# A table of positions in a fused attention and mixture-of-experts kernel: tile 3's columns are turned at position 16, the q/k product of tile 1 moves to 18

## The reference, cut to what matters

```python
# attention, per sequence
q, k, v = split(x @ w_qkv.T)            # 16 heads x 16
q, k = rms_norm(q), rms_norm(k)         # over the 16 of a head
q, k = rope(q), rope(k)
attn = softmax(mask(q @ k.T * scale))   # causal, 512 x 512
x = layernorm(x + (attn @ v) @ w_proj.T)
# feed-forward
normed = x * rsqrt(mean(x * x) + 1e-8) * norm_weight
shared = relu(normed @ sw1 + sb1) @ sw2 + sb2
probs = sigmoid(normed @ router_w.T)
scores, idx = top_k(probs, 2); w = scores / (sum(scores) + 1e-6)
routed = sum over the two experts e of  w_e * (relu(normed @ ew1[e] + eb1[e]) @ ew2[e] + eb2[e])
x = layernorm(x + shared + routed)
```

## Time and profile before

| | us |
|---|---|
| median of 3 runs | 946.98 (946.95 to 947.47) |
| the profiled execution | 943.19 |
| its span, first to last instruction | 941.4 |
| mean granted TensorE clock | 0.986 |
| TensorE busy | 880.8 (94%) |
| VectorE busy | 581.1 (62%) |
| ScalarE busy | 613.8 (65%) |
| GpSimd busy | 433.2 (46%) |

### The profile page before, as it was taken

The page is one execution under the profiler, slowest core; times in us unless marked ns, Lnnn a source line. Parts: engine busy times, 40 slices in busy tenths (PEclk is TensorE's granted clock), DMA queues, the critical chain, the costliest instruction groups (busy, mean ns, idle before and its releaser), DMA issues.

```text
span 941.4 us, 26114 instructions
## 1 busy us (share of the span) xinstructions
PE 880.8 (94%) x9049; PEld 698.1 (74%) x9050; DVE 581.1 (62%) x1206; ACT 613.8 (65%) x1061; POOL 433.2 (46%) x602
## 2 busy tenths in 40 slices
PE   4678999999999979999999999999999999999997
PEld 1444556565555647888888989989899889898886
DVE  8664878989988737784444544444444432437976
ACT  4678988888888767343565655556655454666764
POOL 5342454777868636572234434354434344512311
PEclk8799999999999999999999999999999999999999
DMA  5122142425212256567882122121212111239751
GB/s 178 68 68 68 68 147 91 155 84 198 97 70 75 81 185 226 199 211 264 254 293 73 56 68 67 46 70 54 68 48 76 46 58 48 77 118 291 221 168 56
DMA packets 68705, 112.76 MB, mean 120 GB/s; under 512 B 7728, under 2 KB 46000, under 8 KB 68496
## 3 DMA queue, kind: packets, MB, share of 16 engines
q1 hardware_dynamic: 51248, 77.32, 25.0%
q10 hardware_dynamic: 10896, 16.40, 5.9%
q0 software_dynamic: 6480, 17.97, 5.3%
HBM read 66.58 MB, written 45.08 MB: 119 GB/s over the span
## 4 chain that ended last, share of the span: by engine, by line
PE 68%; POOL 9%; issue 7%; DVE 7%; ACT 7%; DMA 1%; another core or an unknown queue 0%; ACTq 0%; DVEq 0%; POOLq 0%; SPq 0%
PE hb L1884 25%; PE yb L1903 24%; ACT prob L871 3%; PE pv_bank L1668 3%; PE hb L1734 3%; PE yb L1771 3%; PE tr L1754 2%; PE slot L1642 2%; POOL rsum L699 1%; PE ma L1681 1%; POOL rsum L696 1%; POOL xg_rows L740 1%; PE slot L1655 1%; POOL nat L714 1%; PE mb L1818 1%
## 5 line engine op out<-in xcount | busy, mean ns | idle before, releaser
L1043 ACT ACTIVATE hf<-hb,b 128x256 f32<-128x256 f32 (+1 forms) x392 | 154.8, 453 | 205.1 <-PE hb L1884 184.8
L1884 PE MATMUL hb<-xgT,wts 128*128 128x256 f16 (+1 forms) x1872 | 213.3, 263 | 1.7 <-ACT hf L1043 1.4
L1903 PE MATMUL yb<-wts,hh 128*128 x1704 | 210.5, 273 | 0.6 <-DVE hh L1472 0.6
L1472 DVE TENSOR_TENSOR hh<-hf,hh 128x1024 f16<-128x1024 f32 (+1 forms) x98 | 118.8, 1215 | 133.8 <-ACT hh L1048 117.6
L1884 PEld LDWEIGHTS hb<-xgT,wts 128*128 x1872 | 181.3, 98 | 20.8 <-issue 1.2
L806 POOL DMA_INDIRECT y_tok<-yb,dest x71 | 77.7, 1095 | 224.1 <-DVE yb L1484 207.3
L1903 PEld LDWEIGHTS yb<-wts,hh 128*128 128x128 f16 x1704 | 166.4, 98 | 19.3 <-DVE hh L1472 1.0
L871 ACT ACTIVATE prob<-slot 128x1024 f32<-128x1024 f32 x160 | 156.4, 1041 | 34.7 <-PE slot L1655 32.1
L1048 ACT ACTIVATE hh<-hf 128x1024 f16<-128x1024 f32 (+1 forms) x98 | 97.6, 996 | 3.1
L740 POOL DMA_INDIRECT xg_rows<-xnh,sl_i x64 | 74.8, 1168 | 15.5 <-issue 13.1
L1484 DVE SCALAR_TENSOR_TENSOR yb<-yb,b2bc 128x512 f32<-128x512 f32 (+1 forms) x39 | 25.1, 643 | 86.4 <-PE yb L1903 52.0
(11 more groups left out here) (250 smaller groups left out, 1437.6 us busy)
## 6 DMA issues: line engine op xcount, KB each, us to landing
wts<-in_w_all SPq DMA_DIRECT2D x23, 512.0 KB
wts<-y_tok SPq DMA_DIRECT2D x32, 256.0 KB, 4.5
xg<-xg_rows ACTq DMA_DIRECT2D x30, 264.0 KB
stage<-in_w_all SPq DMA_DIRECT2D x12, 512.0 KB
w_split<-chunk_hl SPq DMA_DIRECT2D x12, 512.0 KB
xTf<-in_xT SPq DMA_DIRECT2D x8, 512.0 KB
xin<-in_x SPq DMA_DIRECT2D x8, 512.0 KB
resid<-y SPq DMA_DIRECT2D x16, 256.0 KB
```

What stands on the lines that cost most here:

```text
L1043: act.activation(hf[:, c, 0:size], hb[c // 2][:, (c % 2) * TT:(c % 2) * TT + size], ACT.Relu, bias=bias, scale=1.0 / WS).then_inc(S("relu_ ...
L1472: dve.tensor_tensor(hh[:, par, 1, cs, 0:size], hf[:, cs, 0:size], hh[:, par, 0, cs, 0:size], ALU.subtract).then_inc(S("h_lo"), 1)
L1884: ins = pe.matmul(hb[hc // 2][:, (hc % 2) * TT:(hc % 2) * TT + size], weights(e, c, w, hc * P, P), xgT[:, par, x * DC + c, 0:size], start= ...
L1903: ins = pe.matmul(bank, hh[:, par, x, hc, P * j:P * j + P], weights(e, DC + hc * D // CH, w, hc * D % CH, D), start=(n == 0), stop=(n == H ...
```

## The change

Only numbers in the tables of positions change. For batches 2 to 7, modulo 20: the q/k product of tile 1 goes from 16 to 18 and its rotation from 17 to 19; the roots of tiles 0 and 1 and what follows them (`REFINE`, `QN`) go one position later; the turning of tile 3 goes from 18 to 16, in batch 1 as well; the turning of tile 0 goes from 6 to 7; the rank from 16 to 17 (offset 56 to 57), because the turned k columns of tile 3 now use `mc` at 16; the first scatters and the tables follow by one position.

```diff
-QK = (-28, -24, -20, -16)
-ROPE = (-27, -23, -19, -15)
-ROOT = (-21, -12)
-REFINE = (-20, -11)
+QK = (-28, -22, -20, -16)
+ROPE = (-27, -21, -19, -15)
+ROOT = (-20, -12)
+REFINE = (-19, -11)
 MORE_WEIGHTS = -24
-QN = (-20, -18, -11, -10)
-TR = (-14, -10, -6, -2)
+QN = (-19, -17, -11, -10)
+TR = (-13, -10, -6, -4)
...
-RANK = (56,)
-SCATTER = (58, 59, 61, 63)
+RANK = (57,)
+SCATTER = (59, 60, 61, 63)
...
-SPACED = (58, 60, 64, 66)
+SPACED = (59, 60, 64, 66)
...
-TABLE = NPOS * (NB - 1) + 57
+TABLE = NPOS * (NB - 1) + 58
...
 OPENING = {
...
-    TR: ((-33, -28, -27, -26), (7, 10, 14, 18)),
+    TR: ((-33, -28, -27, -26), (7, 10, 14, 16)),
```

## The result

The changed kernel takes 968.75 us (median of four runs, 967.51 to 974.34) against 946.97 us. The ratio is 1.0243, 95% interval 1.0215 to 1.0271. The prediction named 949.4 us, range 943.0 to 953.4: the sign was right, the size was not, and the time lies outside the range.

What follows compares the result with a forecast made beforehand. Attention windows were taken as set by handovers, VectorE's list closing four of five; the routed experts are TensorE's own. Opening −3.0, windows +4.4, end +1.0 make +2.4 us: 949.4 us median, range 943.0 to 953.4.

Steps and rivals of the forecast that it cites:

- The opening: Second batch's first scores: TensorE's 1.94 us wait for the k copies goes; −3.0 us, bounds −1.2 to −3.6.
- The clock's share of this term: Opening, 82 to 84 us: if the half clock follows from the pause, it goes too; 1.63 us on two products.
- The windows, rotation: Third to seventh batch: tile 1's rotation moves behind the projection on VectorE; +1.20 in four windows, −0.4 in the fifth, sum +4.4.
- the square's wait of 2.5 us: Windows, ScalarE: `sq` (L888) waits for tile 1's `ssq`, one buffer, about 2.5 us, five times.
- the wait for the roots: Windows, VectorE: `nt` (L1176) newly waits for ScalarE's `ry`; 0.75 us taken, 0 to 1.4.
- my loop: Four windows of five: projection, VectorE's list, last attended tile, TensorE, projection; work added on VectorE there costs its full length.
- The windows, GpSimd: Windows, GpSimd: `norms` and two scatters now come ahead of tile 2's swap; left to the first rival.
- POOL becomes the bound: Slower rival, windows: VectorE waits 1.1 to 2.0 us for tile 2's swap; +3.2 us, 952.6; chance 0.26 with the lost opening.
- The end of the stage: End of attention: token count moves behind both early hidden pieces, tables begin 2.45 us later; +1.0 us, between +0.3 and +2.1.
- the operation that I guessed would lose its 1.8 us: L1340 in VectorE's tables, 1.95 us where some 0.15 is due; whatever holds it may be over: −1.8 us.
- VectorE absorbs the move: Faster rival, windows: `nat` regains 0.51 us beside the swap, windows −0.4; total −3.1, 943.9 us; chance 0.32.
- putting rope behind a piece of `shifted`: Windows: by the shared-port rule rope waits about half of `shifted`'s 2.48 us; four windows 5 us dearer, 954.4; counted with slower rival.

Runs made afterwards that it cites:

- rank late with the scatters kept: Kernel before with rank and tables one position later and the scatters at their old positions, first at 58: 1.0049, 947.7 us.
- the scatters of batch 4 apart: Changed kernel with each of batch 4's 8 scatters waiting for the exponentials of batch 7 to reach its place: 1.0192, 963.1 us.
- The change with the scatters kept: Changed kernel with the scatters back at their old positions, from 58, rank and all else staying changed: 1.0169, 959.1 us.

## Why the prediction was wrong, point by point

**The opening** (−3.0 us) was right in place and nearly in size: −2.4 us (0.13 to 0.37%) alone. The pause of the earlier trace rows is gone in the changed kernel; TensorE there:

```profile
82.87 1.46 PE L1681 MATMUL ma<-wqkv,xTh 128*128 128x512 f16 x6 [0.24 <-ACT sq L888]
84.25 2.36 PE L1668 MATMUL pv_bank<-prob,vst 128*32 128x512 f32 x32
```

Both products, 2.69 and 2.76 us in the earlier trace rows, are back at the full clock's lengths. The clock's share of this term (1.63 us) isn't there in every execution: of six profiles with the old opening, all with the pause of 1.94 us, three (rotation late, scatters late, rank late with the scatters kept) have the full clock behind it.

**The windows, rotation** (+4.4 us) had the right mechanism and half the size: +9 us alone. With the changed order around it, and the scatters kept, it is more: 16 us above the kernel before, although that has the opening's gain in it. The order of VectorE, the square's wait of 2.5 us and the wait for the roots came as written. Two pieces were missing. I counted ScalarE's late square as covered by its idle time and overlooked that it holds bank `ma`: TensorE's v product waits for it (1.05 us in the window shown, 5.1 us in five windows; none in these windows before, and 1.8 us in the run with the late rotation alone). And the pause at the attended tile falls on an earlier tile than the one of the earlier trace rows, so my loop, which carried only the last tile's wait, was not the one that closed. That loop also left out TensorE's wait for tile 0's high half, which was as large before (2.8 us in five waits) as the one for `an` (2.8 in four).

**The windows, GpSimd.** Beside the size of the rotation's term, this is the step that failed: the sum gave the scatter's move nothing. "POOL becomes the bound" was a rival with 0.26, priced at +3.2 us by the wait for tile 2's swap alone. That wait came in the changed kernel (1.78 us). The scatter's move costs 19 us by itself, half of it through tile 0's high half, which I had not followed, and 7 us in the changed kernel, of which the run without the stall (the scatters of batch 4 apart) already gives 5 back. The earlier trace rows showed the swap ending at 215.29 and a full queue; what I did not ask is where on GpSimd the scatter had stood before: in idle time, where it was free.

**The price of a pause** was taken as its length. In the changed kernel pauses of 1.6 to 2.5 us at `an` had the lower clock behind them in four windows, and the attended product lost 1.2 to 1.7 us in each (4.05 for 2.36 in the one shown). I had used this at the opening, as a gain, and not in the windows, as a cost.

**The stall at the seventh end** (6 us) was in the profile before, as 3.46 us on ScalarE, and I had no term for it.

**The end of the stage** (+1.0 us) agrees with +1.0 us alone, whose interval (−0.3 to +2.5) can't tell that size from nothing or from twice as much. The count and the tables of the changed kernel, and the operation that I guessed would lose its 1.8 us:

```profile
442.19 0.15 DVE L1330 COPY cum<-mc 1x8 f32<-1x8 f32 x1 [2.50 <-PE mc L1715]
...
443.85 0.15 DVE L1340 SCALAR_TENSOR_TENSOR cum<-seg,iota_e 1x8 f32<-1x8 f32 x1
```

VectorE waits 2.50 us for the count, and L1340 takes 0.15 us, so the 1.8 us did come back: `hh` begins 9.2 us behind the first of these operations where it was 11.3. That the whole change loses 6 us behind the last projection is more than this term; the scatters alone have 3.5 us there (962.1 − 406.5 against 552.1), the late rank with the scatters kept 2.7. What makes these is not shown.

**The rivals.** "VectorE absorbs the move" was wrong. The Trainium skill's rule on the shared port ("SBUF — State Buffer", section "Who interferes with whom") was read in the prediction as putting rope behind a piece of `shifted`; the trace doesn't show that: `rot` at 214.35 takes 0.69 us and `ssq` follows at once, beside `shifted` from 214.54. If one of them was held, it was `shifted`: 2.51 us for two, where two take 1.11 us at 206.46 in the same kernel.

The pieces measured alone are +1.98% (scatters), +0.97% (rotation), +0.49% (rank and tables, scatters kept) and −0.25% (opening), 3.2% together; the change has 2.4%. They don't add up because late scatters and late rotation delay the same tiles: with the rotation late and tile 0 turned later, TensorE does not wait for tile 0's high half in these windows, neither with the scatters late nor with them kept, and taking them back gives 0.7% and not 2.0%. That is also why taking either back in the changed kernel gave so little at first.

No run tests by itself what the title names: tile 3's turning at 16 and tile 1's product at 18 in the windows of the middle. From the runs on record it can only be bounded. The change with the scatters kept has it, the late rotation alone has not, and their distances to the second to seventh end lie 0.3 us apart or less but for one of 1.7 (44.9 against 43.1, with half the clock from 222 to 228 us): 2.6 us in all. By the ratios 1.69 − 0.97 − 0.49 + 0.25, 0.5%, stays without a cause. What else stays open: whether the late rank costs something besides its scatters and tables (1.0049 with the scatters kept, of which its profile has 2.7 us behind the last projection), and what the engines wait for when scatters stand in a row.

## What to carry to other kernels

Follow every instruction that a moved step takes along, above all those on an engine that isn't the bound: a job of less than 2 us that stood in idle time was free, and moving it one position later, behind a wait, cost 2% of the run by itself. When two repairs of a slow kernel each do nothing, test the smallest edit on the fast kernel instead: moving one list alone told in one run what four runs on the changed kernel had not. Then take the same step back in the slow kernel, for its price there is another one: 7 us here for 19 alone. And price a pause of TensorE with what its clock does behind it, not by its length.

## What the runs showed of the hardware that was not expected

While GpSimd issued 8 indirect scatters in one row, ScalarE stood still for 6.01 us (the first 0.9 of them still for the attended product, which ended at 355.7) and VectorE for 5.63, with a releaser that the profile doesn't show; TensorE's matmuls came with pauses of 0.49 and 1.03 us between them, and ScalarE and VectorE went on 1.4 to 1.7 us after the last scatter. With the scatters held apart the distance fell from 41.4 to 33.3 us. Seven in a row had 3.46 us on ScalarE in the kernel before, and no such pause in the change with the scatters kept.

TensorE's half clock after a pause of about 2 us came in the same place in some profiles and not in others: after 1.99 us near 68 us in the changed kernel (0.50 from 70 to 72 us) and not in the kernel before; after 1.94 us at 80.76 in the kernel before (0.50) and not in the late rotation alone, with the same pause at 80.75.
